# Recurrent graph kernel: all loads of stage two from SyncE, x of the gates first; no wait for its own turn in the normalisation of stage one

## The reference, cut to what matters

```
adj = relu(einsum('bn,tnm->btm', x.reshape(b, n*d), masker_param) + masker_bias).reshape(b, t, n, n)
adj = adj / (adj.sum(-1, keepdims=True) + 1e-6)
h = broadcast_to(x[:, None], (b, t, n, d))
m = einsum('btnm,btmd->btnd', adj, h @ weight)
gates = m @ w_ih.T + b_ih + h @ w_hh.T + b_hh
r, z, ng = split(gates, 3)
r = sigmoid(r); z = sigmoid(z); ng = tanh(r * ng)
h = (1 - z) * ng + z * h
# then batch norm over b, layer norm over (t, n, d), a score and a softmax over n, and the weighted sum
```

## Time and profile before

| what | us |
|---|---|
| median of 3 runs | 2257.29 (2251.59 to 2257.75) |
| profiled execution, its time | 2254.87 |
| profiled execution, its span | 2253.1 |
| TensorE busy | 2141.4 (95%) |
| VectorE busy | 1221.3 (54%) |
| ScalarE busy | 866.1 (38%) |
| mean DMA rate | 123 GB/s |

### The profile page before, as it was taken

One profiled execution on the slowest core, in us unless ns is written; L12 is line 12 of the kernel. 1 busy time (PEld: TensorE's weight loads), 2 busy tenths in 40 slices (PEclk: granted clock), 3 DMA queues, 4 the chain that ended last, 5 costly groups with the idle time before them and its releaser, 6 DMA issues. The chain is left out here.

```text
span 2253.1 us, 33249 instructions
## 1 busy us (share of the span) xinstructions
PE 2141.4 (95%) x11694; PEld 1680.5 (75%) x11694; DVE 1221.3 (54%) x2370; ACT 866.1 (38%) x1471; POOL 66.7 (3%) x68
## 2 busy tenths in 40 slices
PE   8999999999999999999999999998988988996898
PEld 7888888888888888888888887776766766775333
DVE  5444334444265443344443453776776766878667
ACT  4211111111033111111110123776876776875862
POOL 0000000000000000000000000100100110110000
PEclk9999999999999999999999999998999998998899
DMA  7321222221254212222202234675556566564660
GB/s 249 140 100 51 93 99 104 99 95 45 104 187 147 105 56 83 99 104 102 101 35 104 104 103 119 160 171 162 150 153 167 137 158 171 141 177 138 196 184 11
DMA packets 148058, 276.08 MB, mean 123 GB/s; under 512 B 11565, under 2 KB 106061, under 8 KB 143053
## 3 DMA queue, kind: packets, MB, share of 16 engines
q1 hardware_dynamic: 129836, 237.53, 34.7%
q10 hardware_dynamic: 18144, 37.69, 5.6%
HBM read 196.01 MB, written 79.17 MB: 122 GB/s over the span
## 5 line engine op out<-in xcount | busy, mean ns | idle before, releaser
L431 PE MATMUL psum<-w_hi,x_lo 128*128 128x500 f32 x2080 | 806.3, 388 | 8.2 <-DVE w_lo L289 8.2
L431 PE MATMUL psum<-w_lo,x_hi 128*128 128x500 f32 (+1 forms) x2080 | 807.8, 388 | 0.0
L431 PE MATMUL psum<-w_hi,x_hi 128*128 128x500 f32 x1920 | 743.2, 387 | 0.0
L340 DVE TENSOR_REDUCE rows<-u 128x10 f32<-128x500 f32 x160 | 107.7, 673 | 741.4 <-ACT u L302 741.3
L302 ACT ACTIVATE u<-psum 128x500 f32<-128x500 f32 x160 | 93.9, 587 | 1048.0 <-PE psum L431 1048.0
L431 PEld LDWEIGHTS psum<-w_hi,x_lo 128*128 128x128 f32 x2080 | 391.0, 188 | 88.8 <-issue 8.2
L431 PEld LDWEIGHTS psum<-w_lo,x_hi 128*128 128x128 f32 (+1 forms) x2080 | 390.8, 188 | 78.1
L431 PEld LDWEIGHTS psum<-w_hi,x_hi 128*128 128x128 f32 x1920 | 360.6, 188 | 72.3
L746 PE MATMUL psum<-adj_sb,xs_sb 100*64 100x100 f32 x2048 | 222.6, 375 | 4.4 <-PEq L148 4.4
L746 PEld LDWEIGHTS psum<-adj_sb,xs_sb 100*64 100x64 f32 x2048 | 154.7, 153 | 55.8 <-issue 39.4
L609 ACT ACTIVATE r_gate<-psum,bias 64x400 f32<-64x400 f32 x256 | 151.2, 591 | 60.5 <-PE psum L773 58.9
(11 more groups left out here) (168 smaller groups left out, 2103.9 us busy)
## 6 DMA issues: line engine op xcount, KB each, us to landing
w_raw<-W SPq DMA_DIRECT2D x140, 500.0 KB, 6.5
adjT<-at SPq DMA_DIRECT2D x160, 320.0 KB, 2.3
adj_sb<-adjT SPq DMA_DIRECT2D x32, 800.0 KB
xs_sb<-xz SPq DMA_DIRECT2D x16, 1600.0 KB
hF<-hC ACTq DMA_DIRECT2D x96, 256.0 KB, 2.9
h<-hF SPq DMA_DIRECT2D x64, 256.0 KB, 4.0
adj_sb<-adjT SPq DMA_DIRECT2D x32, 450.0 KB
xg_sb<-xg ACTq DMA_DIRECT2D x14, 800.0 KB, 17.3
```

Of the source, the lines that this page charges most:

```text
L340: nc.vector.tensor_reduce(rows[:, 0], u[:, c2], AX.X, ALU.add).then_inc(dve_step, 1)
L431: last = nc.tensor.matmul(mm_out(w % 2), a[0:r, w, k, :], b[0:r, k, :], start=k == 0 and n == 0, stop=k == KF and n == 1)
```

## The change

Two edits. In stage one `normalise` loses its parameter `first` and the wait for `at_ready`. In stage two ScalarE no longer issues `xg`: SyncE does, ahead of `adj` and `xs`. For that SyncE no longer waits for the last aggregation of the tile (`ax_done`) but for its last h (`h_ready`), since `xg` is read until then. The number of transfers and their sizes stay as they were.

```diff
         @block.vector
         def _(dve):
-            def normalise(c, c2, first=False):
+            def normalise(c, c2):
...
                 dve.wait_ge(dve_step, 3 * c + 3)
-                if not first:
-                    dve.wait_ge(at_ready, c)
                 nc.vector.tensor_tensor(an[:, :, 0:N], u[:, c2], rows[:, 2].unsqueeze(2).to_broadcast([P, GN, N]),
                                         ALU.mult).then_inc(an_ready, 1)
...
-                            normalise(c - 1, (w - 1) % 2, first=static and it == 0 and w == 1)
+                            normalise(c - 1, (w - 1) % 2)
...
                 for r in range(2):
                     tile = it * 2 + r
                     if more:
-                        sp.wait_ge(ax_done, (tile + 1) * ROUNDS)
+                        sp.wait_ge(h_ready, (tile + 1) * ROUNDS)
+                        load_xg(sp, shared, ins, tile + 2, r)
                         load_adj(sp, shared, adjT, tile + 2, r)
                         load_xs(sp, shared, ins, tile + 2, r)
...
-            def reload_xg(tile, r):
-
-                act.wait_ge(h_ready, (tile - 1) * ROUNDS)
-                load_xg(nc.scalar, shared, ins, tile, r)
...
-                    if q == 0 and (r and more or not r and not (isinstance(it, int) and it == 0)):
-                        reload_xg(it * 2 + r + 1, 1 - r)
```

## The result

| | before | changed |
|---|---|---|
| median of 20 runs each, us | 2255.35 (2244.41 to 2257.75) | 2262.18 (2257.61 to 2267.12) |
| span of the profiled execution, us | 2253.1 | 2265.3 |

The profiled execution of the changed kernel took 2267.09 us and is one of the slowest of its 20, that of the kernel before (2254.87) lies at the median: differences between the two traces are some 5 us larger than between the medians.

A forecast was written before the change was run, and what follows sets the result against it. Stage one was taken as bound by TensorE, stage two by no single engine, with gaps at xg waits and jumps back. Terms 0 - 1 + 38 + 0 = +37 us on 2254.87 gave 2292, range 2264 to 2316.

The forecast's parts named there:

- Stage one bound by TensorE, with or without the wait: Stage one: TensorE's matmuls alone set its length, so it lasts as long as before to 1 us.
- Their round 6 starts later than the loads are in. They keep their time: Stage two, tiles beginning with a jump back: round 6 starts about 34.8 us after the last h, loads in at 32.8; 0.
- the five tiles: Stage two, tiles 4, 6, 8, 10 and 12, where VectorE's hardware loop jumps back: 228.7 us before, change taken as 0.
- rival D: Stage two: the stop at the jump back halves, five tiles fall to 45.0 us, -3.5, 2288; inside the forecast's 0.77.
- Stage one, the wait removed: VectorE's 159 waits for at_ready go: at most 6 us, covered by 5.85 us idle per window; taken as 0.
- The wait that takes the place of the one removed: Stage two: ScalarE's xg wait goes; TensorE waits about 7 us for adj and xs ahead of round 6 in nine tiles.
- 32.8 + 12.2 = 45.0 us a tile: Stage two: loads in 32.8 us after the last h, then 12.2 us from TensorE's restart to the next last h.
- The nine tiles: Stage two, tiles 1, 2, 3, 5, 7, 9, 11, 13, 14, without jump back: 367.0 us before, 405.0 forecast, +38.0.
- ScalarE's issues removed, -1: Stage two: 14 xg issues of 0.36 us leave ScalarE, mostly hidden; bounds 0 and 5 us of gain, 1 taken.
- Rival A: Stage two: loads in after 25.6 us, xg waits simply go, nine tiles at 36.5 us, -38.5, 2215; chance 0.08.
- Rival B: Stage two: loads of 28 to 29.5 us, new stop costs what the xg wait did; about 2255 to 2262; chance 0.05.
- Rival C: Stage two: the jump-back stop grows past 8.1 us, five tiles 8 us more, +40, 2332; chance 0.10 with slower loads.

The follow-up runs named there:

- e1: The kernel before with the stage-one edit alone (VectorE's loop at 670 to 960): 2234.32 us, ratio 0.9923.
- e3: The changed kernel with 47 waits on a long-signalled semaphore added in stage one, putting VectorE's stage-two loop back at 717 to 1007: 2263.82 us, ratio 1.0049.
- e2: The kernel before with the stage-two edit alone, `normalise` and VectorE's code as before: 2264.10 us, ratio 1.0053.
- e5: The kernel before with 81 waits added to VectorE's stage-one code, its stage-two loop at 798 to 1088: 2235.14 us, ratio 0.9908.
- e6: The kernel before with 209 waits added to VectorE's stage-one code, its stage-two loop at 926 to 1216: 2232.98 us, ratio 0.9904.
- e11: e1 with 24 waits added to VectorE's code, its stage-two loop at 694 to 984: 2233.06 us, ratio 0.991.
- e8: e1 with SyncE issuing adj and xs after the last h instead of the last aggregation, xg left to ScalarE: 2242.71 us, ratio 0.9944.
- e9: e1 with xg moved from ScalarE to SyncE, issued after the last h, behind adj and xs: 2253.13 us, ratio 0.9995.
- e4: The changed kernel with SyncE issuing adj after the last aggregation, then xg and xs after the last h: 2167.67 us, ratio 0.9627.
- e10: The kernel before with 128 waits added to VectorE's stage-one code, its stage-two loop at 845 to 1135: 2253.48 us, ratio 0.9991.
- e7: e4 with the 47 waits put back so that VectorE's loop stands at its old place: 2220.20 us, ratio 0.9843.

## Why the prediction was wrong

- **Stage one bound by TensorE, with or without the wait: right.** TensorE's waits for VectorE there are 9.0 us in all against 8.2. In the profiled execution the stage ended 3 us later than before, where 1 us was forecast; e1 and e3, with the same edit there, are within 1.1 us of the kernel before.
- **"Their round 6 starts later than the loads are in. They keep their time", 0 for the five tiles: wrong.** They fell from 228.7 us to 215.5, -13.2. The code moved by 47 instructions and the stop went; but e2 and e3, which keep VectorE's loop in its old place, have 216.4 and 218.5. So 10 to 12 of the 13 us come from the moved loads alone: with the burst starting at the jump the stop there shrinks from 8 us to 2 to 3, with up to 4.8 a round later. That is rival D, which the prediction named and priced at -3.5 with its 32.8; with the loads really in after 30 us it is worth more. That the five could not fall further than the loads allow was right: they ended at 43.1 us each, level with the others.
- **Stage one, the wait removed, "I take 0": wrong in mechanism, small in this sum.** The instruction's own time was 0, that of its place wasn't. 47 instructions fewer moved the stage-two loop off a bad place; alone that is -17 to -22 us (e1, e5, e6, e11), beside the stage-two edit 2 to 4 (e2, e3 against the changed kernel). The prediction said that page borders could move, but put the price at "that of C or D", a longer or a shorter stop, never at a stop gone for good, and gave it no chance of its own.
- **The wait that takes the place of the one removed: right.** xg lands in 5.1 us, ScalarE's wait for it is gone, and TensorE stands ahead of round 6 in all fourteen tiles, eleven times put down to xs. Mechanism and place are as forecast.
- **Its size, 32.8 + 12.2 = 45.0 us a tile: too large, and with the five tiles the step that failed.** The nine tiles took 391.5 us, 43.5 each, +24.5 instead of +38. The restart comes 28.4 to 31.8 us after the last h, 30.4 on average of fourteen, where I had used the one burst at the start of the stage, 32.7, against my own lower bound of 30.6 from the middle burst. That one burst was a long one: the same sequence at the same place took 31.0 us in e2, 31.4 in the changed kernel and 32.6 in e8. Why the later bursts are shorter still stays open. The tail was 12.2 to 13.4, 0.8 us longer than taken.
- **ScalarE's issues removed, -1:** not separable here; no run removes them alone.
- **The range.** 24.5 - 13.2 = +11.3 is what came in the profiled execution, +6.8 in the medians. The prediction worked out almost this case, 2260 with loads in 30.6 us and a shorter stop, and then cut it off at 2264 without a reason. Both departures came together; e2 and e3, with the stop there, lie at 2264, the edge of the range.
- **A slip in reading.** The earlier trace rows end at 2000 us, ahead of the last wait for xg: ScalarE's waits in tiles 1 to 14 are 34.0 us in 8, not 28.4 in 7. No term of the sum uses it.

Rival A was far off, since the loads as issued needed 30 us. Rival B has the time that came, 2255 to 2262, but not for its reason: it asks for loads in 28 to 29.5 us and leaves the five tiles alone. Rival C's condition wasn't met where the stop is kept either: in e3 it is 2.63 + 4.75 = 7.4 us, not over 8.1. The rule of the Trainium skill cited in the prediction on issuing engines held in one respect, the change brought hardly any rate (162 GB/s over tiles 1 to 14 against 159); e1 against e9 speaks for it that the issuing engine can matter for the order all the same.

## What to carry to other kernels

An edit that only removes instructions can change the time at a loop elsewhere on that engine. Look at the jump back of each hardware loop for a gap at "issue", and at the count of instruction fetches on the page, before and after; if the count doubles, shift the code and time it again. And when a burst of loads is late, look at what each transfer waits for and when it is wanted. A transfer whose slot is free early should not wait for the latest one's (adj after the last aggregation turned +0.35% into -3.7%, e4), but one that is wanted late should not go ahead of one that is wanted early (xs ahead of xg, e9, gives all of it back).

## What the runs showed of the hardware

- A loop of 291 instructions on VectorE ran without further fetches at four places of its code (670, 694, 798, 926) and with about five more for each jump back at two others, 717 and 845, that lie 128 apart. The stop at the jump was 7.3 to 9.1 us in the kernel before, e10 and e7, where loads were already on their way, and 2.0 to 2.8 us in e2 and e3, where they started at the jump, with up to 4.8 a round later.
- An idle TensorE costs more than its gap: 8.5 us of idle time made a tile 10 us longer; TensorE's own work in it took 37.93 us instead of 36.40, at a mean granted clock of 0.89 instead of 1.00 (e7 against e4).
- The four kernels with the loop off the bad places have medians of 2233.0 to 2235.1 (e1, e5, e6, e11); e10 has 2253.5, and the kernel before 2251.4 to 2255.4 in the sets timed here. So nothing else in the shifted code matters at this size.
